# A two-layer graph network with experts: the second layer's table in two float32r parts, and where the subtractions stand

## Chip, cores and metric

The kernel runs on 1 core of one Trainium2 chip. The metric is the device time of one execution in microseconds (us), the median of several runs.

## The reference, cut to what matters

There are 6250 nodes with 256 features, 100000 edges sorted by destination, and 8 edge types.

```python
# _L0_gnn_ref: two layers
for l in range(2):
    W = einsum('rb,bio->rio', coeffs[l], bases[l])        # 8 matrices of 256x256
    h = einsum('ni,rio->rno', x, W)                       # each node under each type
    msg = h[edge_type, src] * deg_inv[dst][:, None]
    x_new = segment_sum(msg, dst, num_nodes) + x @ self_loops[l]
    x = relu(x_new) if l == 0 else x_new
# and around it
x = x + gnn(layernorm(x)) + linear_attention(layernorm(x))
x = x + relu(expert MLP of layernorm(x), one expert of 32 per node by argmax)
```

## The kernel before

Nodes are taken in 49 blocks of 128. A layer is computed as a table and a gather. The table of a layer has 50176 rows in DRAM, one for each node and edge type, with the 256 features of the node under that type's matrix. The layer then gathers, for each edge, the row of its source and type, and sums the rows by destination. The edges are sorted by destination, so a block's edges are a stretch of the list. They come in tiles of 128 edges; 4 tiles are a group, there are 782 tiles and 196 groups, and a block takes 4.98 groups on the average, since a group that two blocks share is worked on twice.

`startup` makes the constants, the transposed and normalised nodes `g.xT`, the matrices of both layers, and the table of layer 0. `gnn_first` runs the first layer's gathers and sums, and with each finished block multiplies it by the second layer's 8 matrices and stores the rows of table 1. `gnn_second` runs the second layer's gathers and sums, adds attention, own product and input, and ranks the nodes by expert. `experts` scatters the nodes into buckets, runs them through their experts and scatters the results to the output. The four follow each other, with a barrier between them.

The gather is POOL's alone. `Aggregate.gather` (line 505) issues one indirect DMA a tile (line 515): 128 rows into the ring `gnn_ring`, which has RG = 16 groups of 4 tiles in both layers. From group 16 on, POOL waits before every second group until PE has begun on a group far enough ahead (`pairs`, compared with a value that was worked out from the edges). Each ring place has a semaphore `landed`; SP runs `count` (line 499), which waits for them in order and raises `groups_in`.

The sum is PE's, with VectorE's one-hots. For each half group VectorE compares the destinations of 2 tiles with the block's node numbers (line 542) into `gnn_oh`, which has two halves, `oh_ok` and `oh_free` passing them to and fro; PE waits for `groups_in` and `oh_ok` and multiplies each tile's one-hot by the gathered rows into the bank `gnn_pagg` (line 558). Both are fp32 and stand as two records a tile in the trace. The layer-0 rows have a 257th column of ones, which counts the edges. These loops over the groups of a block are run by the engines, not unrolled (`Fori`).

In `gnn_first` the engines follow these orders, block b at a time, with block b - 1's second product inside. PE: own product of b (line 717), sum of b, keys and values (line 723), their outer product for b - 1 (line 730), product of b - 1 with the 8 matrices in 4 chunks of 512 columns, each of 6 float32r products (line 744), transposes of b (line 751). VectorE: one-hots of b, low part of b - 1 (line 649), keys of b - 1, finish of b (lines 659 to 665), additions of b (lines 669, 670). ACT: transposed x1 of b - 1 out of PSUM and its high part (lines 786, 788), own part of b (line 794), then `store` of b - 1: copy of each chunk out of the bank `gnn_pm` into one of two row buffers (line 800), one DMA of 1 MB into the table (line 808), then the exponentials. The float32r products are exact because an operand is split in a high part, rounded to float32r by a copy, and a low part, the difference. PE's next product waits for `rows_ok`, which the last copy raises. The last block's store goes in two halves.

In `gnn_second` VectorE's `step` (line 917 on) adds the output bias to the input (line 943), multiplies the sum by the inverse degree and adds (line 953), frees the bank, and adds the own and attention products (line 963).

## Time and profile before

| | us |
|---|---|
| median of 3 runs | 2586.64 (2582.43 to 2588.01) |
| span of the profiled execution | 3411.3 |
| PE busy in it | 2398.6 (70%) |
| PE weight loads busy | 1737.8 (51%) |
| POOL busy | 1649.4 (48%) |
| VectorE (DVE) busy | 1074.1 (31%) |
| ScalarE (ACT) busy | 626.8 (18%) |
| HBM read, written | 260.7 MB, 138.9 MB |

The profile is one execution with the hardware profiler on, and here its span is 825 us longer than the median of the plain runs. A duration in it is that of one operation, a gap between two operations can be a wait for another engine, and a row's bracket names what ended it as far as semaphores tell; "issue" means that nothing the profile shows ended it. The busy shares are means over four stages with different limits. In this kernel a copy's `<-DMA pre_bs` or `gnn_ring` in a bracket names a semaphore that has been used again since, and not that transfer.

### The profile page before, as it was taken

How to read it: one execution, taken by the hardware profiler on the slowest of the kernel's cores; microseconds unless marked ns; L12 is line 12 of the kernel's file. 1: busy time of each engine (PE TensorE's matmuls, PEld its weight loads, DVE VectorE, ACT ScalarE, POOL GpSimd, SP SyncE). 2: the span in 40 equal slices, each digit the busy share in tenths (PEclk: the TensorE clock that was granted, in tenths of full speed). 3: DMA queues.
4: the chain of work that ended last, by engine and by line, in shares of the span. 5: the costliest groups of instructions: out<-in, count | busy, mean ns of one | idle time of the engine just before them, and what ended most of it. 6: DMA issues, size and time to landing. Idle time of an engine off the chain costs nothing. (4 is left out here: it accounts for less than half of the span.)

```text
span 3411.3 us, 37691 instructions
## 1 busy us (share of the span) xinstructions
PE 2398.6 (70%) x9525; PEld 1737.8 (51%) x9528; DVE 1074.1 (31%) x3125; ACT 626.8 (18%) x1391; POOL 1649.4 (48%) x1712
## 2 busy tenths in 40 slices
PE   6999357777777777776882766666666666566287
PEld 3788235555555555554561544444444444455065
DVE  3787022222222222222220333333233333234233
ACT  4455101111111111110120011111111211110033
POOL 0000655555555555555506555555655555551645
PEclk9999678888888888888895877777777777788587
DMA  8764433334333333433423332333332223231531
GB/s 225 250 232 192 139 100 123 128 125 133 123 124 124 126 124 125 128 122 112 131 90 93 88 91 87 88 87 88 91 88 84 86 87 90 85 87 32 164 110 54
DMA packets 159887, 397.24 MB, mean 116 GB/s; under 512 B 34926, under 2 KB 92241, under 8 KB 145932
## 3 DMA queue, kind: packets, MB, share of 16 engines
q0 software_dynamic: 81648, 219.65, 22.1%
q10 hardware_dynamic: 35772, 124.12, 9.4%
q1 hardware_dynamic: 42337, 51.93, 5.5%
q8 instruction: 58, 0.95, 0.1%
q14 instruction: 72, 0.59, 0.1%
HBM read 260.70 MB, written 138.94 MB: 117 GB/s over the span
## 5 line engine op out<-in xcount | busy, mean ns | idle before, releaser
L515 POOL DMA_INDIRECT gnn_ring<-table,g_idx x1564 | 1512.7, 967 | 1418.2 <-PE gnn_pagg L558 680.0
L558 PE MATMUL gnn_pagg<-gnn_ring,gnn_oh 128*128 x3904 | 1215.4, 460 | 483.7 <-issue 427.0
L558 PEld LDWEIGHTS gnn_pagg<-gnn_ring,gnn_oh 128*128 128x128 f32 x3904 | 838.0, 228 | 886.9 <-issue 759.7
L542 DVE TENSOR_TENSOR gnn_oh<-gnn_col,g_dst 128x256 f32<-128x256 f32 x976 | 408.9, 426 | 1471.2 <-DVEq L49 1214.0
L800 ACT COPY second_wr<-gnn_pm 128x512 f32<-128x512 f32 x196 | 103.0, 597 | 1107.8 <-DMA pre_bs<-in_L_gnn_bases 992.7
L1054 ACT ACTIVATE gnn_qe<-gnn_pq,gnn_bq 128x128 f32<-128x128 f32 x98 | 36.1, 368 | 1078.0 <-remote 1036.1
L402 PE MATMUL pre_psum<-pre_whigh,pre_high 128*128 128x512 f32 x392 | 159.0, 406 | 13.1 <-DVE pre_low L309 8.1
L336 DVE SCALAR_TENSOR_TENSOR second_wr<-pre_bs,pre_cr,second_wr 128x512 f32<-128x512 f32 x232 | 159.5, 748 | 2.8
L744 PE MATMUL gnn_pm<-gnn_whigh,gnn_high 128*128 128x512 f32 x392 | 157.5, 402 | 3.5 <-issue 2.5
L744 PE MATMUL gnn_pm<-gnn_whigh,gnn_low 128*128 128x512 f32 x392 | 153.8, 392 | 6.8 <-issue 6.7
L744 PE MATMUL gnn_pm<-gnn_wlow,gnn_high 128*128 128x512 f32 x392 | 152.9, 390 | 4.2 <-issue 4.2
L402 PE MATMUL pre_psum<-pre_whigh,pre_low 128*128 128x512 f32 x392 | 154.5, 394 | 0.0
L402 PE MATMUL pre_psum<-pre_wlow,pre_high 128*128 128x512 f32 x392 | 154.0, 393 | 0.0
L717 PE MATMUL gnn_po<-gnn_ws,g_xT 128*128 128x256 f32 x196 | 77.8, 470 | 106.5 <-issue 103.3
L449 ACT COPY pre_rows<-pre_psum 128x512 f32<-128x512 f32 x196 | 114.4, 589 | 124.8 <-PE pre_psum L402 110.0
L1159 POOL DMA_INDIRECT out<-g_xT x80 | 80.0, 1000 | 96.0 <-DVE g_xT L1236 77.8
L1038 PE MATMUL gnn_pnd<-g_kvn,gnn_qf 128*128 128x132 f32 x196 | 42.5, 299 | 82.3 <-issue 80.8
L723 PE MATMUL gnn_pk<-gnn_wkv,g_xT 128*128 128x512 f32 x196 | 99.7, 633 | 0.0
L717 PEld LDWEIGHTS gnn_po<-gnn_ws,g_xT 128*128 128x128 f32 x196 | 41.1, 225 | 113.0 <-issue 110.7
L1153 POOL DMA_INDIRECT bucket<-rt_x,exp_posi x49 | 51.2, 1045 | 87.4 <-DVE exp_posi L1257 72.8
L659 DVE TENSOR_SCALAR gnn_dm<-gnn_pagg 128x1 f32<-128x1 f32 x49 | 7.8, 159 | 268.1 <-remote 213.6
L402 PEld LDWEIGHTS pre_psum<-pre_whigh,pre_high 128*128 128x128 f32 x392 | 74.5, 190 | 29.0 <-DVE pre_low L309 9.7
(174 smaller groups left out, 2382.6 us busy)
## 6 DMA issues: line engine op xcount, KB each, us to landing
table<-pre_rows ACTq DMA_DIRECT2D x49, 1024.0 KB
table<-second_wr ACTq DMA_DIRECT2D x48, 1024.0 KB
gnn_ring<-table,g_idx POOLq DMA_INDIRECT x1564
bucket<-gnn_zrow SPq DMA_DIRECT2D x16, 650.0 KB
g_xT<-bucket SPq DMA_DIRECT2D x20, 520.0 KB, 6.3
pre_bs<-in_L_gnn_bases SPq DMA_DIRECT2D x32, 240.0 KB
pre_bs<-in_L_gnn_bases SPq DMA_DIRECT2D x30, 256.0 KB
x1T<-gnn_x1T ACTq DMA_DIRECT2D x49, 128.0 KB
```

Of the source, the lines that this page charges most:

```text
L336: ins = V.scalar_tensor_tensor(out=w, in0=base[:, n % AT_ONCE, :, :], scalar=cr[:, i:i + 1], in1=w, op0=ALU.mult, op1=ALU.add)
L402: mm = nc.tensor.matmul(psum[:, n, 0:hi - lo], x[i][:, h, :], w[j][:, h, lo:hi], start=(h == i + j == 0), stop=(h == H2 - 1 and i == 1))
L449: nc.scalar.copy(rows[:, b % 2, lo:hi], psum[:, n, 0:hi - lo]).then_inc(chunk_free, 1)
L515: eng.indirect_dma_start(self.ring[:, q % RG, t, 0:D], None, self.g.table[self.l][:, :], bass.IndirectOffsetOnAxis(ap=self.g.idx[:, at:at ...
L542: self.nc.vector.tensor_tensor(self.oh[:, h, :, :], self.col[:, :].unsqueeze(1).to_broadcast([P, n, P]), self.g.dst[:, ds(q * TPG + h * n, ...
L558: mm = nc.tensor.matmul(pagg[:, k, 0:self.width], self.oh[:, h, i, :], self.ring[:, ds(q & (RG - 1), 1), t, 0:self.width].rearrange("p o n ...
L717: mm = nc.tensor.matmul(po[:, 0:D], g.xT[:, h, b * P:(b + 1) * P], ws[:, h, :], start=(h == 0), stop=(h == H2 - 1))
L723: mm = nc.tensor.matmul(pk[:, :], g.xT[:, h, b * P:(b + 1) * P], wkv[:, h, :], start=(h == 0), stop=(h == H2 - 1))
L744: mm = nc.tensor.matmul(pm[:, n, 0:CW], x[i][:, h, :], w[j][:, h, n * CW:(n + 1) * CW], start=(h == i + j == 0), stop=(h == H2 - 1 and i = ...
L800: ins = nc.scalar.copy(rows[:, k, n * CW:(n + 1) * CW], pm[:, n, 0:CW])
L1153: eng.indirect_dma_start(g.bucket[:, :], bass.IndirectOffsetOnAxis(ap=posi[:, b:b + 1], axis=0), r.x2[:, b, :], None).then_inc(scattered, 16)
L1159: eng.indirect_dma_start(out[:, :], bass.IndirectOffsetOnAxis(ap=xb[:, t % XS, D:D + 1].bitcast(I32), axis=0), xb[:, t % XS, 0:D], None, b ...
```

## The change

Table 1 gets rows of 512 floats: for each node and type 256 floats of a high part, rounded to float32r, and 256 of the low part, the rest. Table 0 stays. The second layer's gather brings 2 KB rows, its ring has 8 groups and not 16, its one-hots are float32r, and its sum is one float32r product of 512 columns a tile, which leaves the sum of the high parts in the first and that of the low parts in the second half of the bank. VectorE adds both, in one operation more a block.

In the first layer ACT's copy of a chunk is now the high part. VectorE subtracts it from the chunk, still in PSUM, and writes the low part beside it (`rows_low`, one operation of 128x512 a chunk). Of the 4 subtractions of a block, chunks 0 and 1 stand at the end of VectorE's step, behind the additions and before the next block's one-hots, and chunks 2 and 3 in the next step behind its one-hots. The row buffer has the same size but holds one block and not two: each of its 4 chunks has its own semaphore and its own DMA of 0.5 MB (`send`), 2 at the end of ACT's step and 2 in the next step before `store`. PE's next product waits for the 4 subtractions (`lo_ok`) and not for the copies. For the last two blocks all 4 go together.

```diff
@@ Shared
-        self.table = [dram(f"table{l}", (NP * R, D), F32) for l in range(2)]
+        self.table = [dram(f"table{l}", (NP * R, (1 + l) * D), F32) for l in range(2)]
@@ Aggregate
-        self.width = D + 1 if l == 0 else D
-        self.ring = s.sb("ring", [P, RG, TPG, ROW])
+        self.rg = RG[l]
+        self.row = D if l == 0 else 2 * D
+        self.width = D + 1 if l == 0 else 2 * D
+        self.ring = s.sb("ring", [P, self.rg, TPG, ROW if l == 0 else 2 * D])
         self.col = s.sb("col", [P, P])
-        self.oh = s.sb("oh", [P, HALF, TPG // HALF, P])
+        self.oh = s.sb("oh", [P, HALF, TPG // HALF, P], F32 if l == 0 else F32R)
+        self.tiles = self.ring if l == 0 else self.ring[:, :, :, :].bitcast(F32R)
@@ gather
-                eng.indirect_dma_start(self.ring[:, q % RG, t, 0:D], None, self.g.table[self.l][:, :],
+                eng.indirect_dma_start(self.ring[:, q % rg, t, 0:self.row], None, self.g.table[self.l][:, :],
@@ gnn_first, vector
+            def rows_low(lo, hi):
+                for n in range(lo, hi):
+                    reach(eng, hi_ok)
+                    V.tensor_tensor(rows[:, n, :, 1, :].bitcast(F32R), pm[:, n, 0:CW].rearrange("p (r d) -> p r d", d=D),
+                                    rows[:, n, :, 0, :], ALU.subtract).then_inc(lo_ok, 1)
+
             def step(b, k, prev):
                 agg.onehots(eng, b, seq)
+                if b > 1:
+                    rows_low(EARLY, NC)
                 if prev:
                     low_part(1 - k)
                     keys(1 - k)
@@
                 if b == NB - 1:
                     low_part(k)
+                if prev:
+                    rows_low(0, EARLY if b < NB - 1 else NC)
@@
             keys((NB - 1) % 2)
+            rows_low(0, NC)
@@ gnn_first, tensor
                 if b:
-                    eng.wait_ge(rows_ok, b)
+                    eng.wait_ge(lo_ok, NC * b)
@@ gnn_first, scalar
-            def store(b, k):
-                reach(eng, stored[k], 16)
+            def store(b):
                 for n in range(NC):
+                    reach(eng, stored[n], 16)
                     reach(eng, chunk_ok)
-                    ins = nc.scalar.copy(rows[:, k, n * CW:(n + 1) * CW], pm[:, n, 0:CW])
...
+                    nc.scalar.copy(rows[:, n, :, 0, :].bitcast(F32R),
+                                   pm[:, n, 0:CW].rearrange("p (r d) -> p r d", d=D)).then_inc(hi_ok, 1)
+
+            def send(b, lo, hi):
+                for n in range(lo, hi):
+                    reach(eng, lo_ok)
+                    eng.dma_start(table_rows(g, 1, b)[:, n * 2 * CW:(n + 1) * 2 * CW],
+                                  rows[:, n, :, :, :].rearrange("p r i d -> p (r i d)")).then_inc(stored[n], 16)
@@
+                if b > 1:
+                    send(b - 2, EARLY, NC)
                 if prev:
-                    store(b - 1, 1 - k)
+                    store(b - 1)
                 reach(eng, kt_ok)
                 nc.scalar.activation(ke[:, k, :], kt[:, k, :], ACT.Exp)
                 nc.scalar.activation(kr[:, k, :], kt[:, k, :], ACT.Relu).then_inc(er_ok, 1)
-
+                if prev:
+                    send(b - 1, 0, EARLY if b < NB - 1 else NC)
@@
-            store(NB - 1, (NB - 1) % 2)
+            store(NB - 1)
+            send(NB - 1, 0, NC)
@@ gnn_second, vector
-                    ins = V.tensor_tensor(xb[:, j, :], xb[:, j, :], bo[:, :], ALU.add)
+                    V.scalar_tensor_tensor(out=xb[:, j, :], in0=agg.pagg[:, j, 0:D], scalar=g.dinv[:, ds(n - 1, 1)],
+                                           in1=xb[:, j, :], op0=ALU.mult, op1=ALU.add)
+                    ins = V.scalar_tensor_tensor(out=xl[:, :], in0=agg.pagg[:, j, D:2 * D], scalar=g.dinv[:, ds(n - 1, 1)],
+                                                 in1=bo[:, :], op0=ALU.mult, op1=ALU.add)
@@
-                    ins = V.scalar_tensor_tensor(out=xb[:, j, :], in0=agg.pagg[:, j, 0:D], scalar=g.dinv[:, ds(n - 1, 1)],
-                                                 in1=xb[:, j, :], op0=ALU.mult, op1=ALU.add)
+                    eng.sem_inc(agg.agg_free, 1)
+                    ins = V.tensor_tensor(xb[:, j, :], xb[:, j, :], xl[:, :], ALU.add)
```

## Rows read from the trace of the kernel before

**Rows 1.** The page: the profiled execution's span.

```profile
span 3411.3 us, 37691 instructions
```

**Rows 2.** Windows of the four stages: start:end length, engines, clock, DMA, GB/s.

```profile
0.00:362.00 362.00, 316.81 (x1338) 238.38 (x1338) 224.82 (x485) 174.81 (x317) 9.48 (x24) 0.96 0.66 224
362.00:1783.00 1421.00, 1064.67 (x3913) 750.60 (x3913) 349.90 (x939) 185.87 (x442) 753.36 (x778) 0.85 0.38 120
1783.00:3156.00 1373.00, 858.28 (x3521) 637.65 (x3521) 426.66 (x1521) 201.90 (x432) 755.29 (x782) 0.76 0.29 85
3156.00:3411.00 255.00, 158.86 (x753) 111.14 (x756) 72.72 (x181) 64.25 (x200) 131.22 (x129) 0.72 0.35 110
```

**Rows 3.** Line 515 (gathers), second layer: ns min/median/max; its waits (us, times).

```profile
L515 POOL DMA_INDIRECT gnn_ring<-table,g_idx x782: 943/949/1215, 1783.3 to 3088.7; - x196
...
  PE gnn_pagg L558: 310.9, 49
```

**Rows 4.** Timeline of POOL, second layer: start, us, what, idle before.

```profile
2510.45 0.95 POOL L515 DMA_INDIRECT gnn_ring<-table,g_idx  x1 [7.17 <-PE gnn_pagg L558]
2511.71 0.95 POOL L515 DMA_INDIRECT gnn_ring<-table,g_idx  x1 [0.30 <-issue]
```

**Rows 5.** Timeline of POOL, end of the first layer.

```profile
1705.86 0.95 POOL L515 DMA_INDIRECT gnn_ring<-table,g_idx  x1 [0.30 <-issue]
1783.29 0.95 POOL L515 DMA_INDIRECT gnn_ring<-table,g_idx  x1 [76.48 <-POOLq L573]
```

**Rows 6.** Timeline of PE, first layer, after POOL's last gather.

```profile
1727.49 1.96 PE L723 MATMUL gnn_pk<-gnn_wkv,g_xT 128*128 128x512 f32 x4
...
1736.33 1.98 PE L558 MATMUL gnn_pagg<-gnn_ring,gnn_oh 128*128 x8
...
1747.21 1.96 PE L723 MATMUL gnn_pk<-gnn_wkv,g_xT 128*128 128x512 f32 x4
```

**Rows 7.** Timelines of PE and of ACT, middle of the first layer.

```profile
1045.01 9.52 PE L558 MATMUL gnn_pagg<-gnn_ring,gnn_oh 128*128 x28 [7.09 <-issue]
...
1041.57 0.59 ACT L800 COPY second_wr<-gnn_pm 128x512 f32<-128x512 f32 x1 [8.64 <-DMA pre_bs<-in_L_gnn_bases]
```

**Rows 8.** Timeline of PE, second layer, between two blocks' sums.

```profile
2517.68 1.11 PE L1014 MATMUL gnn_po<-gnn_wo,gnn_turned 128*128 128x256 f32 x4
...
2521.36 0.86 PE L1038 MATMUL gnn_pnd<-g_kvn,gnn_qf 128*128 128x132 f32 x4
```

**Rows 9.** Timeline of POOL, last stage: first and last of 80 row scatters.

```profile
3256.61 1.01 POOL L1159 DMA_INDIRECT out<-g_xT  x1 [28.19 <-DVE g_xT L1236]
...
3403.47 0.99 POOL L1159 DMA_INDIRECT out<-g_xT  x1 [0.30 <-issue]
```

**Rows 10.** Groups by line, mean ns of one: operations nearest to what is changed.

```profile
L542 DVE TENSOR_TENSOR gnn_oh<-gnn_col,g_dst 128x256 f32<-128x256 f32 x976 | 408.9, 426 | 1471.2 <-DVEq L49 1214.0 <-issue 123.7 <-remote 94.3
...
L356 DVE TENSOR_TENSOR pre_wlow<-pre_rows,pre_whigh 128x1024 fp32r<-128x1024 f32 x4 | 4.7, 1220 | 6.5 <-ACT pre_whigh L462 6.5
```

**Rows 11.** Timeline of PE: two float32r products of 512 columns in a row.

```profile
1005.39 0.39 PE L744 MATMUL gnn_pm<-gnn_wlow,gnn_high 128*128 128x512 f32 x1
1005.62 0.39 PE L744 MATMUL gnn_pm<-gnn_whigh,gnn_low 128*128 128x512 f32 x1
```

**Rows 12.** Timelines of DVE and ACT beside rows 6: between two blocks' one-hots.

```profile
1729.49 0.42 DVE L669 TENSOR_TENSOR gnn_kt<-gnn_pk,gnn_bkv 128x256 f32<-128x256 f32 x1 [0.47 <-PE gnn_pk L723]
...
1731.84 0.77 DVE L542 TENSOR_TENSOR gnn_oh<-gnn_col,g_dst 128x256 f32<-128x256 f32 x2 [0.78 <-DVEq L49]
...
1732.69 0.59 ACT L800 COPY second_wr<-gnn_pm 128x512 f32<-128x512 f32 x1 [0.72 <-PE gnn_pm L744]
```

**Rows 13.** The page's DMA queues: packets, MB, share of 16 engines.

```profile
q0 software_dynamic: 81648, 219.65, 22.1%
q10 hardware_dynamic: 35772, 124.12, 9.4%
```

**Rows 14.** Timeline of ACT: last issue of the first layer.

```profile
1779.62 0.33 ACTq L808 DMA_DIRECT2D table<-second_wr  x1
```

More of the change, by code:

```diff
@@ L488, in __init__ @@
         self.groups_in, self.gate, self.ring_ok = sems["groups_in"], sems["gate"], sems["ring_ok"]
-        self.landed = [s.sem(f"landed{j}") for j in range(RG)]
+        self.landed = [s.sem(f"landed{j}") for j in range(self.rg)]
         self.agg_ok, self.agg_free = sems["agg_ok"], sems["agg_free"]
@@ L499, in count @@
     def count(self, eng, between=None):
+        rg = self.rg
         for q in range(NG):
-            eng.wait_ge(self.landed[q % RG], 16 * sum(min(TPG, NT - p * TPG) for p in range(q % RG, q + 1, RG)))
+            eng.wait_ge(self.landed[q % rg], 16 * sum(min(TPG, NT - p * TPG) for p in range(q % rg, q + 1, rg)))
             eng.sem_inc(self.groups_in, 1)
@@ L507, in gather @@
     def gather(self, eng):
+        rg = self.rg
         for q in range(NG):
-            if q >= RG and q % FREE == 0:
-                last = eng.value_load(self.g.reuse[0:1, q + FREE - 1 - RG:q + FREE - RG], min_val=2, max_val=NG + NB)
+            if q >= rg and q % FREE == 0:
+                last = eng.value_load(self.g.reuse[0:1, q + FREE - 1 - rg:q + FREE - rg], min_val=2, max_val=NG + NB)
                 eng.wait_ge(self.pairs, last)
@@ L524, in begin @@
         if self.l == 0:
-            for j in range(RG):
+            for j in range(self.rg):
                 ins = self.nc.vector.memset(self.ring[:, j, :, D:ROW], 1.0)
@@ L558, in sum @@
                     mm = nc.tensor.matmul(pagg[:, k, 0:self.width], self.oh[:, h, i, :],
-                                          self.ring[:, ds(q & (RG - 1), 1), t, 0:self.width].rearrange("p o n -> p (o n)"),
+                                          self.tiles[:, ds(q & (self.rg - 1), 1), t, 0:self.width].rearrange("p o n -> p (o n)"),
                                           start=False, stop=False, skip_group_check=True)
@@ L607, in gnn_first @@
         kept = [s.sem(f"kept{k}") for k in range(2)]
-        stored = [s.sem(f"stored{k}") for k in range(2)]
+        stored = [s.sem(f"stored{n}") for n in range(NC)]
         dve_own = g.dve_own
@@ L825, in step @@
                 nc.scalar.activation(kr[:, k, :], kt[:, k, :], ACT.Relu).then_inc(er_ok, 1)
+                if prev:
+                    send(b - 1, 0, EARLY if b < NB - 1 else NC)
+            for n in range(NC):
+                eng.sem_inc(stored[n], 16)
             for k in range(2):
-                eng.sem_inc(stored[k], 16)
                 eng.sem_inc(kept[k], 16)
@@ L833, in _ @@
                 step(b, b % 2, b > 0)
-            store(NB - 1, (NB - 1) % 2)
+            store(NB - 1)
+            send(NB - 1, 0, NC)
+            for n in range(NC):
+                reach(eng, stored[n], 16)
             for k in range(2):
-                reach(eng, stored[k], 32 if k == (NB - 1) % 2 else 16)
                 reach(eng, kept[k], 16)
```

30 lines of the change are left out of this document (12 added, 18 removed).

## The prediction

> **What bounds the kernel now.** The profiled execution cannot be taken at its face: its span is 3411.3 us [rows 1], the median of the three plain runs 2586.64 us. So the first question is which of the 825 us are missing there. I read the windows by stage first, then the timelines of POOL, PE and ACT in a steady stretch, then the only stretch without gathers.
>
> The windows give four stages [rows 2]: start-up 362 us, first layer 1421, second layer 1373, experts 255. POOL's gathers (line 515) stand 0.95 us each with 0.30 us between them, a pitch of 1.26 us [rows 4]; with the layer's mean of 0.966 us (755.29 us for 782) [rows 2] the pitch is 1.27, so 782 gathers need 993 us a layer. In the trace POOL also waits 310.9 us for PE to free the ring [rows 3], because PE stalls: 7 to 8 us once a block, for no releaser, and ACT stands still in the same microseconds before a copy whose product has long been done [rows 7]. After POOL's last gather of the layer, at 1705.86 [rows 5], these stalls are gone: PE goes from one block to the next in 1747.21 − 1727.49 = 19.72 us, of which 1736.33 − 1727.49 = 8.84 is fixed work and 10.88 the sum of 5 groups, 20 tiles [rows 6]. I take the stalls to belong to the profiled execution. In the second layer the fixed part runs from 2517.68 to 2522.22, 4.54 us [rows 8]; with the sum of rows 6 a block needs 15.42 us of PE. Sixteen gathers need 20.3 us of POOL.
>
> Now the plain run is rebuilt twice. The experts' 80 scatters spread over 147 us where 79 times 1.29 is 102 [rows 9], so that stage is about 210 without stalls. If POOL's pitch is 1.27 in plain runs too: 362 + 993 + 23 (first layer's drain: last landing and group, one fixed part, the last product, the store of 3.7 us between rows 14 and 5) + 993 + 25 (an estimate of the same kind for the second layer's end) + 210 = 2606, 0.8% over the median. If POOL doesn't bind and only PE counts: 362 + 49·19.72 + 18 + about 30 (second layer's lead-in) + 49·15.42 + 20 + 210 = 2362, 225 us short. The first fits. So in plain runs POOL's issue of gathers sets both layers: in the first PE is level with it (19.7 against 20.3), in the second PE has nearly 5 us a block to spare.
>
> **The change part by part.** Second layer, product: today a tile is two fp32 records, 10.88/20 = 0.54 us; it becomes one float32r product of 512 columns, whose starts stand 0.23 us apart [rows 11]. That saves up to 0.31 · 782 = 245 us of PE. With five groups the sum takes between 20 · 0.23 = 4.6 us and today's 10.88 (VectorE's ten one-hots of 0.43 each [rows 10], plus hand-over, lie between), so a block needs 9.1 to 15.4 us of PE. POOL still issues the same 782 gathers: 20.3 us a block. Even with the clock at half all along, 2 · (4.54 + 4.6) = 18.3 is below 20.3. So the saving lands in PE's idle time: 0, but for the last group after the last landing, −1 us.
>
> Second layer, gather: the count stays, the bytes double to 256 KB. Gathers and scatters took 22.1% of 16 engines for 219.65 MB, 3.43 us a MB, the table's writes 9.4% for 124.12, 2.58 us a MB [rows 13]; 0.262 MB take 0.68 to 0.90 us of all 16 engines, under the 1.27 of the issue. What a gather of 2 KB rows costs POOL itself no row shows. The nearest is that an instruction of the scatter kind takes 0.99 and not 0.95 us [rows 9]: bounds 0 to 0.04 · 782 = 31 us; I take 0, for the number of rows is what it was. A gain is excluded, nothing that POOL does gets smaller. The ring falls from 16 to 8 groups, 32 gathers or 40 us ahead; PE waits for data in this layer, never holds more than a block's fixed 4.5 us, so it costs nothing; were PE the slower one, it would still lead by two blocks' sums.
>
> Second layer, VectorE: one addition of 128x256 more a block, 0.43 us [rows 10], behind a sum that PE has finished early: 0, and 0.4 once at the very end, within the −1 above.
>
> First layer, VectorE: four subtractions of 128x512 a block with PSUM as one input. Between 0.43 (256 columns) and 1.22 (1024) [rows 10]: 0.65 each. Two stand behind the one-hots of the next block and before the low part, keys and the sum's finish. Their place is covered: the last one-hot is made over 1 us before the sum ends, so they delay the finish by some 0.5 us, and what waits for it, the transposes, stands behind a product of 24 · 0.23 = 5.5 us. Two stand before the next one-hots. ACT's copy of chunk 1 ends at 1733.28, the subtraction at about 1734.0; from VectorE's release to its first one-hot 1731.84 − 1729.49 = 2.35 us pass today, of which 1.7 without its own two additions, so that the one-hot is made by about 1735.9 to 1736.1; PE reaches the sum at 1736.33 [rows 6, 12]. Cover of 0.2 to 0.4 us: 0, and a subtraction of 1.22 would cost 0.6 us more on two of four, some 0.5 us a block, bound 25 us, part of which POOL's 0.6 us a block of lead takes up.
>
> POOL beside more VectorE work: a gather took up to 1.215 us against a median of 0.949 [rows 3], the mean is 0.017 us over the median, 13 us a layer beside 350 us of VectorE [rows 2, 3]. 196 · 0.65 = 127 us more are 36% more, in proportion 5 us; lower bound 0, upper 196 · 0.27 = 52. I take 3. The Trainium skill, page "SBUF — State Buffer", section "Who interferes with whom", has a rule on this: only a VectorE instruction with two SBUF inputs, or in a two-port mode, gets into GpSimd's way. The subtraction has one input in PSUM, so by that rule the term is 0 and the time 3 us less than mine.
>
> First layer, ACT and DMA: the copies keep their size (0.59 us [rows 12]), the store becomes four sends of 0.5 MB, three more issues of 0.33 us [rows 14] on an engine that is busy 186 of 1421 us [rows 2]. The bytes double to 2.1 MB a block, 5.4 us at 2.58 us a MB, beside 16 gathers of 0.131 MB, 7.2 us: 12.6 of 20.3 us. Hidden. The slots are single now: chunks 2 and 3 are sent just before the store that refills them, some 5 us before their turn, against 1.35 us of data and about 2.3 us of latency.
>
> The end of the layer is not hidden, for no gather runs beside it. Today the last issue is at 1779.62 and the layer ends at 1783.29 [rows 5, 14], 3.7 us for 0.5 MB: 1.35 of data, 2.3 of latency. Afterwards the last block's copies wait until block 47's four sends have landed (from about 1774.3: 5.4 + 2.3, so 1782.0), then copy, subtraction, issue (1.6) and the last block's own 2.1 MB, of which three quarters follow the first send late: 1782.6 + 5.4 + 2.3 = 1790.3. That is +7 us, bounds 3 (landing overlaps the copies chunk by chunk) and 10. The Trainium skill, page "DMA: Bandwidth & Descriptors", section "Anatomy of one DMA — SWDGE (gpsimd) path", fits a DMA at 2.0 us plus bytes over 436 GB/s. As an estimate by that, 2.1 MB take 6.8 us where I have 7.7, twice, and the tail would be +5.
>
> Sum: 2586.64 + 7 + 3 − 1 = 2596 us. In the profiled execution, where PE's stalled block is what POOL waits for (a block takes 1305 / 49 = 26.6 us there [rows 3]), the same change would shorten the span by up to 26.6 − 20.3 = 6.3 us a block, if the stalls stay as they are.
>
> **The rivals.** *Faster: the 0.30 us between gathers belong to the profile.* Then POOL's pitch is 0.97, 15.5 us a block, PE is the bound and the missing 225 us are stalls left in plain runs, 2.3 us a block of 98. A second-layer block goes from 17.7 to POOL's 15.5, which is 49 · 2.2 = 108 us; with the first layer's terms 2487. For it: the layers' PE time is what the page shows busiest. Against: the gap is 0.30 to the digit in both layers and before the scatters, VectorE and PE show no such gap between their instructions, and the rebuilt time falls short by 225. It decides where the pitch is below 15.42 + 2.3 over 16, 1.1 us; between 1.1 and 1.27 nothing is gained.
>
> *Slower by much: the first layer's hand-over breaks its cover.* One-hots late by 0.5 us a block and POOL's gathers longer beside the subtractions: 25 + 20, 2640. For it: cover of 0.2 to 0.4 us only. Against: PE's and POOL's delays share the same slack.
>
> *It doesn't do what it says: the product at 512 columns brings no shorter sum,* since one-hots pace it. The same as my forecast in plain runs, 2596 or less; only the profile would tell.
>
> **How the numbers follow.** Within 0.2%, 5.2 us, counts as no change, about what a measurement can tell here. Forecast 0.62 (tail only 3, no other term: 0.17 of it within 0.2%, 0.45 slower); faster rival 0.24, of it 0.02 within 0.2%; slower rival 0.09; unshortened sum 0.05, with small terms, no change. That gives faster 0.22, no change 0.24, slower 0.54. The forecast's own range is 2588 to 2630 (tail 3, all else 0; or tail 7 and gathers dearer by 31). The whole reaches down into the faster rival, whose gain shrinks with the pitch, to 2530, and up to 2640.
>
> **What would show it.** Right: in the second layer POOL's pitch stays 1.25 to 1.27, its waits for PE fall from 310.9 us to near none, PE's tile goes to about 0.23 us, the second layer's window shortens in the profile from 1373 to about 1070 to 1200 us, while the first layer's ends some 7 us longer after its last gather. Wrong: a plain time below 2580 says that POOL's pitch is smaller without the profile; a pitch above 1.30 in the second layer that the wider row costs POOL; one-hots later than PE's zero product that the cover is gone.

## The result, and the profile after

The changed kernel takes 2605.66 us, the median of four runs (2601.95 to 2608.55), where the kernel before takes 2587.32 (2582.43 to 2588.55): a ratio of 1.007, 95% interval 1.0058 to 1.0082, or 18.3 us. The forecast was 2596, slower, for the reason that POOL's issue of gathers sets both layers. The direction held; the change forecast was 9 us, half of the measured one, and each of its four small terms was off in size or in sign.

The trace of the kernel before on which the forecast rests held stalls [rows 1, 7] that the plain times, 825 us shorter, leave no room for. A second trace of it was taken, its span is 2587.3 us; where the text below gives a number of the kernel before without a group of rows, it is of that second trace. First the page's parts 1, 3 and 5, before, then after.

```profile
span 2587.3 us, 37691 instructions
...
PE 2153.5 (83%) x9525; PEld 1622.6 (63%) x9528; DVE 1074.6 (42%) x3125; ACT 638.6 (25%) x1391; POOL 1640.4 (63%) x1712
...
q0 software_dynamic: 81648, 219.65, 28.6%
...
L515 POOL DMA_INDIRECT gnn_ring<-table,g_idx x1564 | 1504.7, 962 | 703.5 <-issue 473.7
L558 PE MATMUL gnn_pagg<-gnn_ring,gnn_oh 128*128 x3904 | 1053.3, 416 | 291.7 <-PEq L49 240.8
```

```profile
span 2600.2 us, 36299 instructions
...
PE 2008.9 (77%) x8552; PEld 1464.6 (56%) x8552; DVE 1218.1 (47%) x3370; ACT 634.1 (24%) x1391; POOL 1647.9 (63%) x1712
...
q0 software_dynamic: 106672, 322.15, 42.1%
...
L521 POOL DMA_INDIRECT gnn_ring<-table,g_idx x1564 | 1511.9, 967 | 705.7 <-issue 472.8
L564 PE MATMUL gnn_pagg<-gnn_ring,gnn_oh 128*128 x2928 | 866.0, 436 | 442.5 <-PEq L50 410.7
...
L683 DVE TENSOR_TENSOR second_wr<-gnn_pm,second_wr 128x512 fp32r<-128x512 f32 x196 | 130.7, 687 | 120.9 <-ACT second_wr L818 120.9
```

PE is 145 us less busy, its idle time before the sum's products rises from 291.7 to 442.5, and the span grows. What stays is POOL's group: 1564 gathers, 0.962 and then 0.967 us each, with 473 us of gaps in both (0.30 each). The busiest engine of the page, PE with 83%, isn't the bound; an engine shown with 63% is, because its gaps belong to its work.

The windows by stage of the two traces (length, then PE, PEld, DVE, ACT and POOL busy, PEclk, DMA share, GB/s): second layer before, first and second layer after.

```profile
1378.00:2398.00 1020.00, 774.47 (x3521) 602.29 (x3521) 431.50 (x1531) 201.89 (x432) 752.24 (x783) 0.88 0.40 117
```

```profile
358.00:1384.30 1026.30, 926.44 (x3913) 686.00 (x3913) 477.14 (x1152) 196.75 (x444) 756.45 (x782) 0.98 0.66 218
1384.30:2410.40 1026.10, 636.29 (x2545) 448.16 (x2545) 449.58 (x1583) 202.01 (x432) 755.46 (x783) 0.74 0.74 216
```

Both layers now take 1026 us. In the second PE is busy 636 of them, at a mean granted clock of 0.74. What it does with its time is plain from its timeline in the middle of that layer:

```profile
2005.76 1.17 PE L564 MATMUL gnn_pagg<-gnn_ring,gnn_oh 128*128 x4
2007.53 1.18 PE L564 MATMUL gnn_pagg<-gnn_ring,gnn_oh 128*128 x4 [0.60 <-issue]
2009.27 1.19 PE L564 MATMUL gnn_pagg<-gnn_ring,gnn_oh 128*128 x4 [0.56 <-PEq L50]
2013.00 1.19 PE L564 MATMUL gnn_pagg<-gnn_ring,gnn_oh 128*128 x4 [2.54 <-PEq L50]
2017.90 2.07 PE L564 MATMUL gnn_pagg<-gnn_ring,gnn_oh 128*128 x4 [3.72 <-PEq L50]
2019.78 0.23 PE L571 MATMUL gnn_pagg<-g_zero 128*128 128x2 bf16 x1
2019.87 2.05 PE L1041 MATMUL gnn_po<-gnn_wo,gnn_turned 128*128 128x256 f32 x4
```

The first three groups were waiting in the ring and are summed at once; the last two come at the pace at which POOL delivers, 4.9 us a group (four gathers of 1.25 us are 5.0), and PE idles before them. After 3.72 us of idling its clock is down at the 1.2 GHz level (the granted clock is 0.50 from 2016 to 2020 us and was 1.00 from 2006 to 2011): four products take 2.07 us and not 1.19, and the four of line 1041 2.05 where the same four took 1.11 in the kernel before [rows 8]. None of this is on the path while gathers still run.

**Where the 18 us are.** POOL's timeline gives every trace four lengths: the first gather of a layer to the end of its last, and what lies between this end and POOL's next work.

```profile
1347.40 0.95 POOL L515 DMA_INDIRECT gnn_ring<-table,g_idx  x1 [0.30 <-issue]
1377.46 0.94 POOL L515 DMA_INDIRECT gnn_ring<-table,g_idx  x1 [29.12 <-POOLq L573]
...
2367.06 0.95 POOL L515 DMA_INDIRECT gnn_ring<-table,g_idx  x1 [0.30 <-issue]
2397.83 2.01 POOL L1153 DMA_INDIRECT bucket<-rt_x,exp_posi  x1 [29.83 <-DVE exp_posi L1257]
```

```profile
1351.64 0.94 POOL L521 DMA_INDIRECT gnn_ring<-table,g_idx  x1 [0.30 <-issue]
1384.31 0.94 POOL L521 DMA_INDIRECT gnn_ring<-table,g_idx  x1 [31.73 <-POOLq L580]
...
2376.84 1.00 POOL L521 DMA_INDIRECT gnn_ring<-table,g_idx  x1 [0.30 <-issue]
2410.40 2.01 POOL L1180 DMA_INDIRECT bucket<-rt_x,exp_posi  x1 [32.56 <-DVE exp_posi L1284]
```

Read so, the thirteen traces other than the first give this table (us; a star stands where that part of the kernel is wholly that of the changed one; in the three runs marked "half" the second layer has fewer gathers and its columns say nothing here; the names are those of the experiments below):

| trace | gathers, 1st layer | its end | gathers, 2nd layer | its end |
|---|---|---|---|---|
| b0, before | 990.1 | 29.1 | 990.5 | 29.8 |
| b1, before | 988.5 | 27.6 | 989.5 | 30.1 |
| after | 994.5* | 31.7* | 993.5* | 32.6* |
| a2, after | 994.9* | 31.8* | 991.7* | 32.0* |
| s1, first layer alone | 994.2* | 32.7* | 989.6 | 30.2 |
| s2, second layer alone | 990.1 | 28.3 | 992.6* | 31.7* |
| s3, product alone | 988.5 | 27.6 | 991.9 | 30.4 |
| p1, no subtractions | 992.1 | 31.2 | 990.7 | 30.1 |
| p2, high parts sent | 993.5 | 31.0 | 988.1 | 30.1 |
| p3, wide rows alone | 987.8 | 27.4 | 995.5 | 31.9 |
| h1, before, half | 990.1 | 27.7 | | |
| h2, after, half | 991.2* | 32.0* | | |
| h3, small one-hots, half | 994.3* | 31.8* | | |

Means of the starred against those of the layer as it was before: 993.8 (5 traces) against 989.2 (6), +4.6; 32.0 (5) against 28.0 (6), +4.0; 992.6 (3) against 990.1 (6, s3 among them), +2.5; 32.1 (3) against 30.1 (6), +2.0. Together 13.1 us. The experts take as long as before (2410.4 to 2600.2 is 189.8, 2397.8 to 2587.3 is 189.5).

### The profile page after: what moved, and what is told of

Same layout as the page of the kernel before. It is cut to its first block and busy times, and to the rows that moved or that the text cites. A ratio compares the mean times of both kernels' runs of the same rounds, so it can differ in the third digit from the quotient of the medians.

```text
span 2600.2 us, 36299 instructions
## 1 busy us (share of the span) xinstructions
PE 2008.9 (77%) x8552; PEld 1464.6 (56%) x8552; DVE 1218.1 (47%) x3370; ACT 634.1 (24%) x1391; POOL 1647.9 (63%) x1712
## 3 DMA queue, kind: packets, MB, share of 16 engines
q0 software_dynamic: 106672, 322.15, 42.1%
## 5 line engine op out<-in xcount | busy, mean ns | idle before, releaser
L564 PE MATMUL gnn_pagg<-gnn_ring,gnn_oh 128*128 x2928 | 866.0, 436 | 442.5 <-PEq L50 410.7
L564 PEld LDWEIGHTS gnn_pagg<-gnn_ring,gnn_oh 128*128 128x128 f32 x2928 | 560.0, 207 | 703.0 <-issue 620.5
L548 DVE TENSOR_TENSOR gnn_oh<-gnn_col,g_dst 128x256 f32<-128x256 f32 (+1 forms) x976 | 408.2, 427 | 816.5 <-DVEq L50 810.3
L818 ACT CAST second_wr<-gnn_pm 128x512 fp32r<-128x512 f32 x196 | 115.0, 587 | 789.5 <-PE gnn_pm L762 789.5
L683 DVE TENSOR_TENSOR second_wr<-gnn_pm,second_wr 128x512 fp32r<-128x512 f32 x196 | 130.7, 687 | 120.9 <-ACT second_wr L818 120.9
L1041 PE MATMUL gnn_po<-gnn_wo,gnn_turned 128*128 128x256 f32 x196 | 96.2, 644 | 0.0
L403 PEld LDWEIGHTS pre_psum<-pre_whigh,pre_low 128*128 128x128 f32 x392 | 74.4, 190 | 16.6
L403 PEld LDWEIGHTS pre_psum<-pre_wlow,pre_high 128*128 128x128 f32 x392 | 74.5, 190 | 14.5
L762 PEld LDWEIGHTS gnn_pm<-gnn_whigh,gnn_low 128*128 128x128 f32 x392 | 73.6, 188 | 16.0
```

The source lines that it names most:

```text
L403: mm = nc.tensor.matmul(psum[:, n, 0:hi - lo], x[i][:, h, :], w[j][:, h, lo:hi], start=(h == i + j == 0), stop=(h == H2 - 1 and i == 1))
L548: self.nc.vector.tensor_tensor(self.oh[:, h, :, :], self.col[:, :].unsqueeze(1).to_broadcast([P, n, P]), self.g.dst[:, ds(q * TPG + h * n, ...
L564: mm = nc.tensor.matmul(pagg[:, k, 0:self.width], self.oh[:, h, i, :], self.tiles[:, ds(q & (self.rg - 1), 1), t, 0:self.width].rearrange( ...
L683: V.tensor_tensor(rows[:, n, :, 1, :].bitcast(F32R), pm[:, n, 0:CW].rearrange("p (r d) -> p r d", d=D), rows[:, n, :, 0, :], ALU.subtract) ...
L762: mm = nc.tensor.matmul(pm[:, n, 0:CW], x[i][:, h, :], w[j][:, h, n * CW:(n + 1) * CW], start=(h == i + j == 0), stop=(h == H2 - 1 and i = ...
L818: nc.scalar.copy(rows[:, n, :, 0, :].bitcast(F32R), pm[:, n, 0:CW].rearrange("p (r d) -> p r d", d=D)).then_inc(hi_ok, 1)
```

## The experiments

**Before, once more.**

> The kernel before, once more, for a trace to set beside that of after. Theory 1 (POOL's issue of gathers sets both layers): no stalls of PE without a releaser, POOL's gathers follow each other at 1.27 us in both layers with no wait for PE, and each layer's 782 gathers take 993 us as in the kernel after; the span is about 2585. The difference of 18 us to after then stands behind the last gathers: the first layer's end about 7 us shorter than after's 31.7, the second's a few. Theory 2 (PE's sums bind the layers): POOL waits for PE in the second layer, and its gathers take over 993 us.

Measured 2589.0 us, span 2587.3, POOL's mean pitch 1.267 us, the gathers 990 us a layer and not 993. The profile puts 7 of POOL's gaps down to PE, 2.1 us in all, but each of them is 0.30 us, as long as the others; no gap between two gathers of a layer is over 0.32 us in this trace or in that of after (there 11 such gaps, 3.4 us). The 825 us that the first trace had more were of that execution. Rebuilding the plain time from pieces of a disturbed trace had given 1.27 and 2606; the second trace confirms both the pitch and the bound. The expectation missed the first layer's end: it is 2.6 us shorter than after's 31.7, not 7.

**The first layer alone.** The changed first layer and the doubled table; the second layer gathers the high parts only and sums in fp32.

```diff
-                eng.indirect_dma_start(self.ring[:, q % RG, t, 0:D], None, self.g.table[self.l][:, :],
+                eng.indirect_dma_start(self.ring[:, q % RG, t, 0:D], None, self.g.table[self.l][:, :].rearrange("n (t d) -> (n t) d", d=D),
...
+            seq(V.tensor_scalar(g.idx[:, :], g.idx[:, :], 1, None, ALU.logical_shift_left))
```

> The first layer's part alone: table of two parts, copies to float32r, subtractions, four sends of 0.5 MB; the second layer gathers only the high parts (rows of 1 KB, indices doubled once between the layers), with the fp32 sum and 16 groups of before. The low parts are left out of the sum. Theory 1: +7 to +13 us, all of it between the first layer's last gather and the second layer's first, and both layers' gathers 993 us. Rival (subtractions get in the way of PE's first layer or of POOL's issue): +20 or more, with the first layer's gathers above 1000 us.

Measured 2598.39 us, ratio 1.0051 (1.0037 to 1.0064). In the trace the first layer's gathers take 994.2 us and its end 32.7, the second layer is untouched. The time is as expected, the place is not: against the means of before the gathers take 5.0 us more and the layer's end 4.7, where all of it was expected at the end. Two thirds or more of the loss arise in the first layer, the part of the change that was to prepare the gain.

**The second layer alone.** The first layer of before; the second gathers pairs of neighbouring rows, 2 KB an index, makes float32r one-hots, one product of 512 columns and the additional addition.

```diff
+            if self.l:
+                table = table.rearrange("(n t) d -> n (t d)", t=2)
...
+            seq(V.tensor_scalar(g.idx[:, :], g.idx[:, :], 1, None, ALU.logical_shift_right))
```

> The second layer's part alone: rows of 2 KB, 8 groups, float32r one-hots, one product of 512 columns, one addition more; the first layer and its table are those of before, so that each gathered row is the pair of rows that holds the wanted one, and the sums are of other values than the reference's. Theory 1: 0 to +8 us, the second layer's gathers stay at 993 us. Rival 1 (PE binds the second layer): -50 us or more. Rival 2 (a row of 2 KB costs POOL more to issue): pitch above 1.28 us and +10 us or more.

Measured 2592.91, ratio 1.0027 (1.0018 to 1.0036). The half that holds the whole of the intended gain makes the kernel slower by itself.

**The product alone.** Before, with float32r one-hots and rows in the second layer, one product of 256 columns: PE's saving without a byte more.

```diff
-        self.oh = s.sb("oh", [P, HALF, TPG // HALF, P])
+        self.oh = s.sb("oh", [P, HALF, TPG // HALF, P], F32 if l == 0 else F32R)
+        self.tiles = self.ring if l == 0 else self.ring[:, :, :, :].bitcast(F32R)
```

> PE's saving alone: the kernel before with float32r one-hots and the second layer's gathered rows read as float32r in one product of 256 columns; rows of 1 KB, 16 groups, nothing else changed, the rows' low bits are left out. PE's sum of a tile falls from 0.54 us to under 0.25. Theory 1: 0, within 3 us of before, for PE only waits longer. Theory 2 (PE binds): about -100 us or more.

Measured 2587.21, ratio 1.0008 (0.9999 to 1.0017). In the second layer from 1400 to 2360 us PE is busy 518 us where it was 746, and POOL 729.6 where it was 729.3. A cut of 228 us in the busiest engine is worth nothing.

**The cover taken away.** If POOL's issue is what covers the saving, fewer gathers must bring it out. In both kernels half of the second layer's gathers are left out.

```diff
+    def tiles_of(self, q):
+        n = min(TPG, NT - q * TPG)
+        return min(n, TPG // 2) if self.l and q >= 16 else n
...
-            for t in range(min(TPG, NT - q * TPG)):
+            for t in range(self.tiles_of(q)):
```

> Before, but in the second layer half of the gathers from the seventeenth group on are left out (the last two tiles of each group are summed from what lies in the ring, so the output differs): 424 gathers for POOL to issue and not 782, all else as before. Theory (POOL's issue sets the second layer, PE stands close behind): POOL would need only 424 x 1.267 = 537 us, so PE becomes the bound at 15.4 us a block, 756 us and some lead-in, and the time falls by about 220 us, to 2370. Rival (something other than POOL's issue, PE or the landing of the data, already sets the layer): less than 50 us gained. If nothing but POOL mattered, 453 us would go.

Measured 2380.3 us, 205 less than before (ratio 0.921, 0.9189 to 0.9232). PE now sets the pace; its timeline has no stop but 0.8 us at each block's start:

```profile
1604.60 0.17 PE L569 MATMUL gnn_pagg<-g_zero 128*128 128x2 bf16 x1
...
1609.75 10.54 PE L562 MATMUL gnn_pagg<-gnn_ring,gnn_oh 128*128 x40 [0.82 <-issue]
1620.12 0.17 PE L569 MATMUL gnn_pagg<-g_zero 128*128 128x2 bf16 x1
```

1620.12 − 1604.60 is 15.52 us a block; the forecast had 15.42 from [rows 6, 8].

> The changed kernel with the same half of the second layer's gathers left out (same tiles summed from what lies in the ring). Theory (the saving of PE is real and only covered by POOL): now PE's shorter sums show; a block of PE is 9.1 to 15.4 us, POOL's share 10.8 us, so the layer takes 540 to 620 us, the time falls to some 2170 to 2240 and is 130 to 200 us under the kernel before with the same gathers left out. Rival (the one-hots pace the sum, so the single product brings nothing): within 20 us of that kernel, about 2370.

Measured 2345.53 us (ratio 0.9076, 0.9056 to 0.9096): only 35 us under h1, far from the 130 to 200 expected. The saving is covered twice. PE's timeline of one block, and VectorE's beside it, say by what:

```profile
1616.35 0.17 PE L561 MATMUL gnn_pagg<-g_zero 128*128 128x2 bf16 x1
1618.25 1.26 PE L568 MATMUL gnn_pagg<-gnn_ring,gnn_oh 128*128 x4 [1.73 <-issue]
1620.19 1.20 PE L568 MATMUL gnn_pagg<-gnn_ring,gnn_oh 128*128 x4 [0.68 <-SPq L512]
1622.06 1.19 PE L568 MATMUL gnn_pagg<-gnn_ring,gnn_oh 128*128 x4 [0.67 <-PEq L50]
1623.95 1.19 PE L568 MATMUL gnn_pagg<-gnn_ring,gnn_oh 128*128 x4 [0.70 <-PEq L50]
...
1630.99 0.17 PE L561 MATMUL gnn_pagg<-g_zero 128*128 128x2 bf16 x1
```

```profile
1621.16 0.89 DVE L552 TENSOR_TENSOR gnn_oh<-gnn_col,g_dst 128x256 fp32r<-128x256 f32 x2 [0.98 <-DVEq L50]
1623.02 0.89 DVE L552 TENSOR_TENSOR gnn_oh<-gnn_col,g_dst 128x256 fp32r<-128x256 f32 x2 [0.98 <-DVEq L50]
```

PE needs 1.2 us for a group and begins one every 1.87 to 1.89. VectorE makes the two one-hots of a group in 0.89 us and then stands for 0.98 in `take` (line 50, the hand-over of semaphores), 1.87 in all. How much of the 0.98 is the hand-over itself and how much the wait for PE to give a half of `gnn_oh` back, the trace doesn't part: the two engines pass the halves round in a ring, and PE begins each group within 0.04 us of the end of VectorE's pair. In h1 a group took 10.54 / 5 = 2.1. So what the product gives, 4 · 0.54 = 2.1 down to 4 · 0.27, stops at 1.87.

**The second cover made thinner.** h2 again, with one-hot instructions of 32 of 128 columns.

```diff
-                self.nc.vector.tensor_tensor(self.oh[:, h, :, :], self.col[:, :]...
+                w = P if self.l == 0 else P // 4
+                self.nc.vector.tensor_tensor(self.oh[:, h, :, 0:w], self.col[:, 0:w]...
```

> As the changed kernel with half of the second layer's gathers left out, but each one-hot instruction of the second layer writes 32 of 128 columns (the others keep what was set once), so the output differs. Theory (VectorE's loop over the one-hots, 0.89 us of work and 0.98 us between, paces the sum at 1.87 us a group): a group falls by some 0.5 us, a block from 14.6 to about 12 us, the time by 100 to 130 us, to 2215 to 2245. Rival (PE's own loop and the hand-over of the semaphores pace it): within 20 us of 2345.

Measured 2301.02 us, 45 less than h2. The rival (within 20 us) falls, but the size expected, 100 to 130, was too large as well. A one-hot instruction fell from 0.43 to 0.23 us, not to the quarter, 0.4 us less a group, and PE's groups went from 1.87 to between 1.54 and 1.63:

```profile
1625.95 1.20 PE L573 MATMUL gnn_pagg<-gnn_ring,gnn_oh 128*128 x4 [1.73 <-issue]
1627.49 1.20 PE L573 MATMUL gnn_pagg<-gnn_ring,gnn_oh 128*128 x4 [0.34 <-PEq L50]
```

The one-hots pace the sum down to about 1.55; there PE's own 1.20 us and 0.34 us of hand-over are nearly all of it.

**Subtractions or doubled writes?** Two variants of s1: without the subtractions but with the doubled table sent (p1), and with the subtractions but the high parts alone sent (p2).

```diff
-                    V.tensor_tensor(rows[:, n, :, 1, :].bitcast(F32R), pm[:, n, 0:CW]..., rows[:, n, :, 0, :], ALU.subtract).then_inc(lo_ok, 1)
+                    eng.sem_inc(lo_ok, 1)
```

> The first layer of the changed kernel alone (second layer and its fp32 sum as before, reading the high parts), with the subtractions left out: VectorE only hands the semaphore on, the low parts in the table are never computed, the doubled table is still sent. Theory (VectorE's subtractions lengthen POOL's gathers and hold the last product): the first layer's gathers go back from 994 to 990 us and the time to 1.002 of before, the rest being the last sends. Rival (the doubled writes do it): gathers stay at 994 us and the ratio at 1.004 to 1.005.

```diff
-                    eng.dma_start(table_rows(g, 1, b)[:, n * 2 * CW:(n + 1) * 2 * CW],
-                                  rows[:, n, :, :, :].rearrange("p r i d -> p (r i d)")).then_inc(stored[n], 16)
+                    eng.dma_start(table_rows(g, 1, b)[:, n * CW:(n + 1) * CW].rearrange("p (r d) -> p r d", d=D),
+                                  rows[:, n, :, 0, :]).then_inc(stored[n], 16)
```

> The first layer of the changed kernel with its subtractions, but only the high parts are sent, four sends of 0.25 MB a block into a table of the old size; second layer as before. Theory (VectorE's subtractions): gathers of the first layer stay at 994 us, ratio 1.002 to 1.004. Rival (the doubled writes): gathers at 990 us, ratio 1.000 to 1.002.

p1: ratio 1.0022 (1.0013 to 1.0031), gathers 992.1. p2: ratio 1.0033 (1.0021 to 1.0045), gathers 993.5. Neither theory has it alone. With the subtractions and without the doubled bytes the gathers take nearly the full 993.8 us, the other way round they stand between this and 989.2; the untouched traces of the first layer scatter from 987.8 to 990.1 (of the second from 988.1 to 991.9), so p2's 993.5 is clear and p1's 992.1 only just. Both variants have the four sends and the changed hand-over too, and no run has these alone.

The traces say more than the totals. With the start and end of every gather set against those of VectorE's instructions, the gathers of the first layer (all but the first) fall into groups; the last column adds up what they take over 0.946 us each:

| gathers that overlap, of VectorE | trace | count | mean, us | longest | over 0.946 in all, us |
|---|---|---|---|---|---|
| nothing | b0 | 211 | 0.946 | 0.955 | −0.1 |
| a one-hot, low part or key product | b0 | 423 | 0.971 | 1.891 | 10.4 |
| nothing | p2 | 89 | 0.946 | 0.949 | 0.0 |
| subtractions only | p2 | 97 | 0.945 | 0.949 | −0.1 |
| a one-hot, low part or key product | p2 | 457 | 0.978 | 1.896 | 14.7 |

The last kind are this layer's instructions with both inputs in SBUF; the gathers left over (148 and 139) overlap VectorE's other instructions, with means of 0.960 and 0.955 us. A gather beside a subtraction is as short as one beside an idle VectorE; so it is in all six traces that have subtractions, 583 such gathers with a longest of 0.951 us. What grows is the time beside the other kind: 8.6 to 10.6 us in the six untouched traces, 12.1 in p1, 14.7 in p2, 12.0 to 15.5 in the five of the changed layer; the means, 9.7 and 14.5, differ by 4.8, as much as the 4.6 us sought. So the subtraction doesn't hold POOL; that it and the writes move VectorE's other instructions against the gathers is the likely way, which no run shows. A one-hot and a subtraction, each with its gather, from p2:

```profile
1004.74 0.43 DVE L542 TENSOR_TENSOR gnn_oh<-gnn_col,g_dst 128x256 f32<-128x256 f32 x1 [0.44 <-DVEq L49]
1004.96 1.03 POOL L515 DMA_INDIRECT gnn_ring<-table,g_idx  x1 [0.30 <-issue]
...
1021.31 0.69 DVE L677 TENSOR_TENSOR second_wr<-gnn_pm,second_wr 128x512 fp32r<-128x512 f32 x1 [1.74 <-ACT second_wr L812]
...
1021.50 0.95 POOL L515 DMA_INDIRECT gnn_ring<-table,g_idx  x1 [0.30 <-issue]
```

Both variants also have 3 us of the 4 at the layer's end (31.2 and 31.0 against 28.0), but not the same 3; the part on the forecast takes them apart.

**Wide rows alone.** Before, with 2 KB for each index in the second layer, a ring of 8 groups and the fp32 sum of the first 256 columns.

```diff
-        self.width = D + 1 if l == 0 else 2 * D
+        self.width = D + 1 if l == 0 else D
```

(against s2; one-hots and VectorE's part of the second layer are those of before.)

> Before, but the second layer gathers pairs of neighbouring rows, 2 KB for each index, into a ring of 8 groups; the fp32 sum reads the first 256 columns (other rows than before where the index is odd, so other values), VectorE as before. Theory (the wider gather costs POOL a little): second layer's gathers at 993 us against 990, ratio 1.001 to 1.002. Rival (what VectorE does more in the second layer, and the float32r one-hots, cost it): gathers at 990 us, ratio 1.000.

Measured 2590.29, ratio 1.0024 (1.0013 to 1.0034), by the intervals as much as s2's 1.0027; gathers 995.5, more than the 993 expected, the end 31.9. What the second layer loses comes with the wide rows and their ring of 8 groups; the two weren't parted, but no gap of POOL between gathers is over 0.32 us, so it never waited for the ring. Line by line (min/median/max ns, then the time from issue to landing), before and then p3:

```profile
L515 POOL DMA_INDIRECT gnn_ring<-table,g_idx x782: 942/946/1219, 1377.5 to 2367.1; - x196
...
DMA to landing us min/median/max: 2.7/2.8/3.7
```

```profile
L524 POOL DMA_INDIRECT gnn_ring<-table,g_idx x782: 942/946/1220, 1374.5 to 2369.0; - x196
...
DMA to landing us min/median/max: 3.4/3.7/6.0
```

The median gather costs POOL the same 0.946 us; more of them are among the longer ones (145 of 782 over 0.96 us against 106), and each lands 0.9 us later. The landing shows only once, after the last gather. Of p3's gathers 197 overlap nothing of VectorE: mean 0.945 us, longest 0.955, as in b0 (180, 0.946, 0.952). So 2 KB rows by themselves don't hold POOL; the longer gathers stand beside VectorE's instructions here too.

**After and before again.**

> The changed kernel again, for a second trace and a narrower ratio. Expected: ratio 1.006 to 1.008; first layer's gathers 993 to 995 us, second layer's 992 to 994; from the last gather of the first layer to the first of the second 31.5 to 33 us where the kernel before has 27.5 to 29.5; from the last gather of the second layer to the first scatter of the experts 32 to 33 us against 30. If these four add up to less than 10 us the difference lies elsewhere.

Measured 2603.4 us, ratio 1.0068 (1.0055 to 1.0081), with a trace like the first: gathers 994.9 and 991.7 (0.3 under the range expected), ends 31.8 and 32.0.

> The kernel before once more, for a third trace of it: the traces so far give 13 us between the two kernels where the medians give 18 to 19. If single executions scatter by 2 to 4 us, this one's span lies between 2580 and 2586 us and its four parts (first layer's gathers, its end, second layer's gathers, its end) add up to 2 to 4 us less than in the second trace; if the traces leave out something real, the span is 2587 us again and the difference lies in no part.

Measured 2584.29 us, span 2582.6, its four parts 3.8 us less than b0's, as expected from scatter. The two traces of before have 2587.3 and 2582.6, the two of after 2600.2 and 2600.6: 15.5 us between their means, of which the four parts hold 13.1 by the table's means. The medians of plain runs differ by 18.3 and 18.8. The rest, some 2 us of the traces and 5 of the medians, has no place in the four parts; start-up alone scatters by several us (the first gather stands at 357.2 and 358.3 before, at 358.0 and 361.2 after). It stays open.

## Why the forecast held in direction and not in size

**The bound: right.** POOL's pitch is 1.267 us in an undisturbed trace (1.27 forecast from a disturbed one), no gap between two gathers of a layer is over 0.32 us in either kernel, and s3 puts PE's saving at zero in plain time. The faster rival, on which 0.24 stood, needed a pitch below 1.1. Two of the signs named for being right could not tell: the 310.9 us of waits for PE and the window of 1373 us belonged to the disturbed execution, and b0 has neither.

**Product of a tile: its worth right, its size in part.** Zero in the plain time, as said. Within PE, the step "a block needs 9.1 to 15.4 us" holds only at its upper end: 14.64 in h2 (1616.35 to 1630.99), since the one-hots and their hand-over pace the sum, which the forecast named as a rival that would change nothing. Starts of products of 512 columns stand (1.20 − 0.39) / 3 = 0.27 us apart in the sum, not 0.23.

**The gather of 2 KB rows: failed, +2.5 and not 0.** The forecast had bounds of 0 and 31 and chose 0, "for the number of rows is what it was". The nearest row named there, 0.04 us on every instruction, isn't what happened either: the median stays at 0.946 us, and the gathers beside an idle VectorE are as short with 2 KB rows as with 1 KB (p3). The page counts 81648 packets on q0 before [rows 13] and 106672 after, 25024 / 782 = 32 more a gather; they don't lengthen such a gather. The added time stands beside VectorE's instructions, a meeting of the two that the forecast priced in the first layer only; which way the wide rows bring it about isn't shown. s3, without wide rows, had 991.9 us, so the ranges with and without wide rows overlap (991.7 to 993.5 and 988.1 to 991.9), and the 2.5 is the weakest of the four differences. The other half of the step, DMA under the issue, was right: no gather waits.

**POOL beside more VectorE work: the mechanism failed, and the size, +4.6 and not 3, came near by luck.** The forecast let the subtractions lengthen the gathers in proportion to VectorE's busy time. They take 0.687 us each (0.65 forecast), but gathers that overlap only them take 0.945 to 0.948 us, as beside an idle VectorE. The Trainium skill, page "SBUF — State Buffer", section "Who interferes with whom", says that only a VectorE instruction with two SBUF inputs, or in a two-port mode, hinders GpSimd; the subtraction has one input in PSUM. The traces agree with the rule, by the 583 gathers above, and nearly all long gathers (119 of the 124 over 0.96 us in p2) overlap an instruction with two SBUF inputs. What the forecast drew from the rule, a term of 0, doesn't follow all the same: the layer's gathers took 4.6 us more, beside instructions that were there before.

**The first layer's end: +4.0 and not +7.** The step that failed is "the last block's copies wait until block 47's four sends have landed". They don't wait. (In that sum 1782.0 and 1.6 also make 1783.6 and not 1782.6, so that by its own terms it was +8.) ACT's timeline after shows the last block's copies one product apart, with nothing between but the product:

```profile
1372.38 0.59 ACT L818 CAST second_wr<-gnn_pm 128x512 fp32r<-128x512 f32 x1 [1.97 <-PE gnn_pm L762]
1373.75 0.59 ACT L818 CAST second_wr<-gnn_pm 128x512 fp32r<-128x512 f32 x1 [0.79 <-PE gnn_pm L762]
...
1376.48 0.59 ACT L818 CAST second_wr<-gnn_pm 128x512 fp32r<-128x512 f32 x1 [0.78 <-PE gnn_pm L762]
1376.51 2.87 ACTq L824 DMA_DIRECT2D table<-second_wr  x4
```

From the end of the last copy, 1377.07, to the first gather, 1384.31, pass 7.2 us; before, from 1373.77 to 1377.46, 3.7. p1, without subtractions, has the same 7.2 and p2, with half the bytes, 5.6: 1.9 of the 3.5 us come with the order of the last block, four sends that stand on ACT behind all four copies (the kernel before sends its first half after the second copy), 1.7 with the doubled bytes, and none with the subtraction. The subtraction costs its 0.7 us one step earlier: PE's last product begins 0.87 us after block 47's last copy and not 0.14 (0.20 in p1). What is left is where POOL's last gather falls: it ends 1.9 us before the last sum begins in b0 and 0.2 in after, so that this pair differs by 2.6 us at the layer's end and the means by 4.0. The estimate that the forecast had from the Trainium skill, page "DMA: Bandwidth & Descriptors", section "Anatomy of one DMA — SWDGE (gpsimd) path", +5, came out nearer, but by luck: it was made for the same two waits, of which one isn't there, and the page's fit is for DMAs that POOL issues, while these are ACT's. For 0.5 MB the fit gives 3.2 us as an estimate; the sends of after land 3.5 us after their issue at the median.

**The second layer's end: failed in sign, +2.0 and not −1.** What was not in the sum: the last gather lands 0.9 us later, and PE, idle before the last group, enters the end at the 1.2 GHz level (granted clock 0.50 from 2381 to 2384 us, where b0 has 1.00 from 2366 to 2373): the last group and the two products behind it, before and after:

```profile
2370.72 1.99 PE L558 MATMUL gnn_pagg<-gnn_ring,gnn_oh 128*128 x8 [1.01 <-PEq L49]
...
2372.58 1.11 PE L1014 MATMUL gnn_po<-gnn_wo,gnn_turned 128*128 128x256 f32 x4
2373.52 1.03 PE L1016 MATMUL gnn_po<-gnn_ws,gnn_x1T 128*128 128x256 f32 x4
```

```profile
2381.17 2.07 PE L564 MATMUL gnn_pagg<-gnn_ring,gnn_oh 128*128 x4 [1.08 <-PEq L50]
...
2383.13 2.06 PE L1041 MATMUL gnn_po<-gnn_wo,gnn_turned 128*128 128x256 f32 x4
2384.98 1.61 PE L1043 MATMUL gnn_po<-gnn_ws,gnn_x1T 128*128 128x256 f32 x4
```

Four products of float32r at the low level take 2.07 us where eight of fp32 at the high level took 1.99: at this place the saving is gone. Between these two traces, which differ by 2.8 us here, the last sum ends 5.2 and not 4.5 us after POOL's last gather (+0.7), the products behind it take 3.3 and not 1.8 us (+1.5), and most of the rest lies in VectorE's chain, which has one addition more. With p3 the same end takes 31.9 us on another way: PE is at the high level there and is late with the fp32 sum of the last block. The forecast's "−1 us for the last group" took the duration of a busy PE for an idle one.

**The first layer's hand-over: right.** The one-hots' cover held: PE's idle time before the first layer's sums went from 75.2 to 84.4 us, 0.2 a block, and none of it reached POOL; the slower rival (2640) is excluded.

**The sum.** +4.6 + 4.0 + 2.5 + 2.0 = 13.1 where the forecast had +3 + 7 + 0 − 1 = 9; of the measured 18.3 some 5 us were in neither. The tail was taken 3 us too long and the other three terms 7 us too short together, so that 9 is as near as it is because these offset each other. The measured time lies in the forecast's range of 2588 to 2630, whose upper end stood on 31 us for wide rows that cost 2.5.

## What to carry to other kernels

Before an engine is relieved, find the one that never waits for a producer, gaps between its instructions included: its count times its pitch, set against the stage, says what a saving elsewhere can bring, here nothing for 228 us of PE. If such a saving is bought with bytes, work on other engines or a longer last block, these costs fall where no cover exists: here 6 us at the ends of two stages and 7 us in the bounding engine's own instructions, where they overlap another engine's. For the latter, look which instructions the long ones overlap before blaming the work that was added. And take the cover away in an experiment before counting on what is under it: a second cover, here the one-hots, may lie below the first.

## What was not expected of the hardware

- One profiled execution of this kernel lasted 3411 us, two others 2587 and 2583. In the long one PE and ACT stood still together for 7 to 8 us a block while gathers ran [rows 7]. What made it isn't known.
- A gather that overlaps no instruction of VectorE, or only one with an input in PSUM (the subtraction), takes 0.945 to 0.948 us in the mean in every trace and never over 0.96. In the first layer at least 85 in 100 of the longer ones overlap an instruction with both inputs in SBUF.
- A gather of 128 rows costs POOL 0.946 to 0.949 us at the median whether the rows have 1 or 2 KB; the landing goes from 2.8 to 3.7 us.
- PE, which idled 2.54 and then 3.72 us between groups, went to the low clock level (granted clock 0.50): four products took 2.07 us and not 1.19. A lighter load on PE is paid back in part by its clock: the layer's mean went from 0.88 to 0.74.
- Two engines that pass two halves of a buffer round pay for it: VectorE stands 0.98 us between two pairs of one-hots, waits for PE and hand-overs together, longer than the work itself, 0.89.
